# A new issue order for the first six periods of a cross-attention and expert kernel, with fewer dummy matmuls, a later weight load, two sums on GpSimd and a joined router operand

## The chip, the cores and the metric

The kernel runs on one core of a Trainium2 chip. The metric is the device time of one execution in microseconds (us), lower is better; the trace is one profiled execution of the program.

## The reference

There are 8 batches of 256 tokens of width 128. Each goes through a cross-attention with 8 heads of 16 channels, whose softmax runs over the heads and not over the keys, and through a layer of 8 experts of which the two with the highest logits are weighted in.

```python
# attention, q from _layernorm(x), k and v from ctx_1024
scores = einsum('bhqd,bhkd->bhqk', q, k) / sqrt(16)
attn = softmax(scores, axis=1)            # over the 8 heads
ctx = einsum('bhqk,bhkd->bhqd', attn, v)
x = x + ctx @ W_O.T
# experts, on xn = _layernorm(x)
logits = xn @ Wr + br
gates = softmax(top-2 of logits)
h = relu(einsum('btd,edh->bteh', xn, W1) + b1)      # 8 experts, 128 -> 256
x = x + einsum('bte,bteh,ehd->btd', gates, h, W2) + gates @ b2
```

## The kernel before

Each engine runs a list of steps that is written out by hand; semaphores tie the lists together, and nothing reorders them. A batch passes through a pipeline of six stages. In period i, batch i gets its k projection, batch i-1 its q and v, batch i-2 its scores and batch i-3 the rest of its attention, and batches i-4 and i-5 their experts. From period 6 on all engines loop over `period(i)`; the first periods are a list of their own, `beginning()`, on each engine.

Scores come in four units `u` per batch of 128 keys by 128 queries by 8 heads. One unit takes these steps. TensorE's `scores` (or `first_scores` for batch 0) fills one of two buffers `score_ps`; VectorE's `head_max` takes the maximum over the heads; TensorE's `subtract_max` adds its negative; ScalarE's `exponentiate` writes `e_sb`. The sum over heads is made by TensorE with an identity for the four units of batch 0 (`head_sum`, line L351, eight matmuls) and by GpSimd for all others (three additions, L1152 to L1157). ScalarE's `invert_sum` takes logarithm and exponential, VectorE's `normalize` (L911) multiplies. After four units TensorE's `attend_values` and `project_out` follow, then VectorE's `add_residual` and `ln2`, ScalarE's `make_x1n`, TensorE's `transpose_x1n`, `x1T_hi` and `x1T_lo`, and `route` and `expert_up`.

From batch 1 on the heads have to be laid out anew over the partitions. That goes through DRAM on SyncE's queue: `spill_k` writes k and its low part to `k_scratch`, `load_k_stack` reads it into `k_stack`; `spill_q` and `load_q_stack` do the same for q. `scores(b, 0)` waits for both stacks. On the same queue lie the loads of the expert weights w1 (1 MB) and w2 and of the rest of ctx. SyncE issues in program order, and a wait at the head of its list holds all that follows.

w1 is split in a high and a low part: ScalarE's `split_w1(e)` casts, GpSimd's subtracts. `expert_up(0, e)` waits for both. `route` makes the logits from three matmuls for each of two token tiles. `keep_warm(n)` issues n dummy matmuls on the identity (L265). `ln1` makes layer-norm statistics of x on VectorE, and `ln1_rest` finishes them on GpSimd; in the list they stand in five calls, for batches 0, 1, 2, 3 and 4 together, and 5 to 7 together.

## Time and profile before

| what | value |
|---|---|
| median of 3 runs | 211.72 us (211.19 to 213.55) |
| profiled execution | 210.83 us |
| its span, first to last instruction | 209.0 us |
| TensorE busy | 199.0 us, 95% of the span |
| VectorE busy | 166.0 us, 79% |
| ScalarE busy | 132.3 us, 63% |
| GpSimd busy | 110.0 us, 53% |
| granted TensorE clock, mean | 1.000 (2.4 GHz) |

Some 1.8 us of the profiled execution lie outside its span. A busy TensorE need not run at its peak: ends of matmuls are modelled, and one group's busy time reaches a little into the next group's start. The loop over periods starts on TensorE at 81.44 us, with the transposes of batch 5; of batches 0 and 1 the `beginning` lists hold the most, and each later period takes some 22 us.

### The profile page before, as it was taken

The page shows a single profiled execution, that of the slowest core. Times are in us where ns is not written, and L with a number is a line of the kernel's source. Part 1 is how long each engine was busy: PE and PEld are TensorE (multiplying, and loading weights), DVE is VectorE, ACT ScalarE, POOL GpSimd, SP SyncE. Part 2 cuts the span into 40 slices and gives each one's busy share as a digit, 9 for nine tenths or more (in the row PEclk, how much of TensorE's full clock was granted, in tenths as well). Part 3 has the DMA queues.
Part 4 walks back from the last instruction along what each step waited for, and adds up shares of the span by engine and source line. Part 5 has one row for each costly group of instructions (what it writes and reads, how often), then busy time and mean ns, then how long its engine had stood idle before and what let it go on. Part 6 is the DMA issues. An engine that isn't in the chain of part 4 may idle for free.

```text
span 209.0 us, 4976 instructions
## 1 busy us (share of the span) xinstructions
PE 199.0 (95%) x1752; PEld 176.3 (84%) x1752; DVE 166.0 (79%) x445; ACT 132.3 (63%) x316; POOL 110.0 (53%) x132
## 2 busy tenths in 40 slices
PE   6999888698999999999999999999999999999994
PEld 6846775686899889997999799988998999789993
DVE  5398779889789999988888988798989978365542
ACT  2236847796578858687668767575767685345541
POOL 8603657869795475439661966285738672010000
PEclk9999999999999999999999999999999999999999
DMA  6549695725434233424241306050000000000000
GB/s 195 137 137 291 178 266 161 206 86 159 109 102 100 78 100 105 102 75 104 98 106 53 124 14 183 13 175 4 0 3 25 0 2 28 0 3 2 28 0 25
DMA packets 20248, 18.70 MB, mean 89 GB/s; under 512 B 1760, under 2 KB 18688, under 8 KB 20224
## 3 DMA queue, kind: packets, MB, share of 16 engines
q1 hardware_dynamic: 17472, 16.91, 28.2%
q10 hardware_dynamic: 2752, 1.48, 2.7%
q8 instruction: 14, 0.23, 0.4%
q14 instruction: 10, 0.08, 0.1%
HBM read 11.83 MB, written 6.55 MB: 88 GB/s over the span
## 4 chain that ended last, share of the span: by engine, by line
PE 91%; DVE 3%; ACT 2%; issue 1%; POOL 1%; DVEq 0%; POOLq 0%; ACTq 0%
PE y_ps L416 28%; PE h_ps L403 21%; PE score_ps L343 7%; PE misc_ps L362 6%; PE score_ps L331 6%; PE h_ps L351 4%; PE score_ps L265 3%; PE misc_ps L300 2%; PE misc_ps L383 2%; PE score_ps L320 2%; PE score_ps L403 2%; PE misc_ps L371 1%; PE misc_ps L270 1%; PE misc_ps L309 1%; PE misc_ps L289 1%
## 5 line engine op out<-in xcount | busy, mean ns | idle before, releaser
L670 ACT ACTIVATE hT<-h_ps,b_sb 128x256 f32<-128x256 f32 x118 | 49.4, 470 | 34.5 <-PE h_ps L403 33.4
L416 PE MATMUL y_ps<-w_sb,hT 128*128 128x128 f32 x512 | 68.4, 276 | 0.0
L416 PEld LDWEIGHTS y_ps<-w_sb,hT 128*128 128x128 f32 x512 | 63.3, 191 | 3.4 <-issue 2.0
L1152 POOL TENSOR_TENSOR half_sum<-e_sb 128x512 f32<-128x512 f32 x28 | 36.9, 1320 | 34.0 <-ACT e_sb L642 33.6
L911 DVE TENSOR_TENSOR attn<-e_sb,e_rcp 128x1024 f32<-128x1024 f32 x32 | 42.8, 1341 | 3.5 <-ACT e_rcp L653 3.3
L903 DVE TENSOR_REDUCE shift_m<-score_ps 128x128 fp32r<-128x1024 f32 x32 | 38.7, 1213 | 2.4 <-PE score_ps L331 1.2
L403 PE MATMUL h_ps<-x1T_hi,w_lo 128*128 128x256 f32 x118 | 37.7, 320 | 1.3 <-ACT hT L670 0.6
L642 ACT ACTIVATE e_sb<-score_ps 128x1024 f32<-128x1024 f32 x32 | 32.8, 1024 | 5.4 <-PE score_ps L343 5.2
L974 DVE SCALAR_TENSOR_TENSOR acc<-y_ps,gates,acc 128x128 f32<-128x128 f32 x96 | 29.0, 343 | 8.3 <-PE y_ps L416 6.9
L403 PE MATMUL h_ps<-x1T_lo,w_hi 128*128 128x256 f32 x118 | 33.1, 280 | 0.0
L403 PE MATMUL h_ps<-x1T_hi,w_hi 128*128 128x256 f32 x118 | 33.0, 279 | 0.0
L1154 POOL TENSOR_TENSOR quarter_sum<-half_sum 128x256 f32<-128x256 f32 x28 | 27.5, 982 | 2.2
L403 PEld LDWEIGHTS h_ps<-x1T_hi,w_lo 128*128 128x128 f32 x118 | 22.3, 189 | 4.3 <-issue 2.0
L403 PEld LDWEIGHTS h_ps<-x1T_lo,w_hi 128*128 128x128 f32 x118 | 22.4, 190 | 0.3
L403 PEld LDWEIGHTS h_ps<-x1T_hi,w_hi 128*128 128x128 f32 x118 | 22.3, 189 | 0.0
L343 PE MATMUL score_ps<-shift_m,neg_ident 128*128 128x512 f32 x64 | 21.5, 417 | 0.0
L331 PE MATMUL score_ps<-q_stack,k_stack 128*128 128x256 f32 x112 | 19.6, 299 | 1.1 <-issue 1.1
L1157 POOL TENSOR_TENSOR e_sum<-quarter_sum 128x128 f32<-128x128 f32 x28 | 16.6, 592 | 2.2
L1163 POOL TENSOR_TENSOR ln_rstd<-ln_var,neg_half 128x2 f32<-128x2 f32 x8 | 5.7, 708 | 21.2 <-DVE ln_var L870 21.2
L331 PEld LDWEIGHTS score_ps<-q_stack,k_stack 128*128 128x128 f32 x112 | 15.1, 190 | 1.5 <-issue 1.5
L362 PE MATMUL misc_ps<-attn,v_pad 128*32 128x256 f32 x256 | 15.5, 382 | 0.6 <-issue 0.6
L362 PEld LDWEIGHTS misc_ps<-attn,v_pad 128*32 128x32 f32 x256 | 7.7, 109 | 5.9 <-issue 1.0
(113 smaller groups left out, 286.8 us busy)
## 6 DMA issues: line engine op xcount, KB each, us to landing
k_scratch<-k_parts SPq DMA_DIRECT2D x14, 256.0 KB, 2.6
k_stack<-k_scratch SPq DMA_DIRECT2D x14, 256.0 KB, 4.0
q_stack<-q_scratch SPq DMA_DIRECT2D x28, 128.0 KB, 2.7
q_scratch<-q_parts SPq DMA_DIRECT2D x7, 256.0 KB, 2.5
w_sb<-in_w SPq DMA_DIRECT2D x1, 1024.0 KB, 6.5
out_y<-y_out SPq DMA_DIRECT2D x8, 128.0 KB, 1.9
x_all<-in_x ACTq DMA_DIRECT2D x1, 768.0 KB, 6.0
ctxT<-in_ctx_t SPq DMA_DIRECT2D x1, 640.0 KB, 5.5
```

The costliest lines, as they stand in the source:

```text
L331: mm = nc.tensor.matmul(score_ps[:, u % 2, 2 * j * P:(2 * j + 2) * P], k_stack[:, b % 2, j, kt * P:(kt + 1) * P], q_stack[:, b % 2, j, :, ...
L343: mm = nc.tensor.matmul(score_ps[:, u % 2, half * BANK:(half + 1) * BANK], neg_ident[:], m4, start=False, stop=True, skip_group_check=True)
L362: mm = nc.tensor.matmul(misc_ps[32 * g:32 * g + 32, 0:S], v_pad[:, b % 4, kt, h, :], attn[:, b % 2, kt, h, :], start=(odd == 0 and kt == 0 ...
L403: mm = nc.tensor.matmul(hidden(j)[:, c * S:(c + 1) * S], w[:, e, c * P:(c + 1) * P], xt[:, b % 2, :], start=(k == 0), stop=(k == 2))
L416: mm = nc.tensor.matmul(y_ps[:, j % 2, t * D:(t + 1) * D], hT[:, j % 2, c, t * P:(t + 1) * P], w2_sb[:, e * HC + c, :], start=(c == 0), st ...
L642: nc.scalar.activation(e_sb[:, u, :], score_ps[:, u % 2, :], ACT.Exp, scale=SCALE).then_inc(exp_made, 1)
L670: op = nc.scalar.activation(hT[:, j % 2, c, :], hidden(j)[:, c * S:(c + 1) * S], ACT.Relu, bias=b1_sb[:, e * HC + c:e * HC + c + 1])
L903: nc.vector.tensor_reduce(shift_m[:, u % 2, :], score_ps[:, u % 2, :].rearrange("p (h q) -> p q h", h=H), AX.X, ALU.max).then_inc(max_made, 1)
L911: nc.vector.tensor_tensor(attn[:, b % 2, kt, :, qt * P:(qt + 1) * P], e_sb[:, u, :].rearrange("p (h q) -> p h q", h=H), e_rcp[:, u, :].uns ...
L974: op = nc.vector.scalar_tensor_tensor(out=dst, in0=y_ps[:, j % 2, t * D:(t + 1) * D], scalar=gates[:, b % 2, t, e:e + 1], in1=src[:, t, :] ...
L1152: nc.gpsimd.tensor_tensor(half_sum[:], e[:, 0:HQ // 2], e[:, HQ // 2:HQ], ALU.add).then_inc(sum_step, 1)
L1154: nc.gpsimd.tensor_tensor(quarter_sum[:], half_sum[:, 0:HQ // 4], half_sum[:, HQ // 4:HQ // 2], ALU.add).then_inc(sum_step, 1)
```

## The change

The `beginning` lists of TensorE, ScalarE, VectorE and GpSimd are in a new order. Beside that:

- `keep_warm` issues 8, 2 and 1 dummies in place of 12, 5, 1 and 2.
- SyncE loads w1 behind the q stack of batch 1, not ahead of the k stack.
- `PE_SUMS` names the units 1 and 3 of batch 0; the sums of units 0 and 2 go to GpSimd.
- The router's weights stand side by side in `wr_pair`. One matmul of 16 columns and one of 8 take the place of three of 8, and `take_logits` on VectorE adds the two halves in a second instruction. This holds for all eight batches.
- `ln1` and `ln1_rest` are called once for each batch, eight times in all; those of batches 5 to 7 stand much later in the list.
- The transposes of batch 5 in period 6 wait for `v_taken` in place of `b2_added`.

```diff
-    PE_SUMS = 4
+    PE_SUMS = (1, 3,)
...
             spill_k(1)
-            sp.dma_start(w1_sb[:], w1.rearrange("e d h -> d e h")).then_inc(w1_in, 16)
             load_k_stack(1)
             spill_q(1)
             load_q_stack(1)
+            sp.dma_start(w1_sb[:], w1.rearrange("e d h -> d e h")).then_inc(w1_in, 16)
             spill_k(2)
...
                 for t in range(TT):
-                    tok = slice(t * P, (t + 1) * P)
-                    for k, (xt, w) in enumerate(((x1T_hi, wr_lo), (x1T_lo, wr_hi), (x1T_hi, wr_hi))):
-                        mm = nc.tensor.matmul(misc_ps[:, S + t * E:S + (t + 1) * E], xt[:, b % 2, tok], w[:],
-                                              start=(k == 0), stop=(k == 2), skip_group_check=True)
+                    tok, at = slice(t * P, (t + 1) * P), S + 2 * t * E
+                    nc.tensor.matmul(misc_ps[:, at:at + 2 * E], x1T_hi[:, b % 2, tok], wr_pair[:].rearrange("p k e -> p (k e)"),
+                                     start=True, stop=False, skip_group_check=True)
+                    mm = nc.tensor.matmul(misc_ps[:, at:at + E], x1T_lo[:, b % 2, tok], wr_pair[:, 0, :],
+                                          start=False, stop=True, skip_group_check=True)
...
-                    transpose_xn(coming, b2_added, coming - 3)
+                    transpose_xn(coming, *((v_taken, 5) if i == 6 else (b2_added, coming - 3)))
...
             def beginning():
+                project_v(0, None, 0)
                 project_k(0, None, 0)
-                project_v(0, None, 0)
-                keep_warm(5)
+                keep_warm(2)
                 transpose_xn(0, None, 0)
                 keep_warm(1)
                 project_q(0, xnT_taken, 1)
+                project_v(1, v_taken, 1)
                 project_k(1, k_first_made, 1)
-                keep_warm(2)
                 first_scores(0)
...
-            keep_warm(12)
+            keep_warm(8)
...
-                                        br_sb[:].unsqueeze(1).to_broadcast([P, TT, E]), ALU.add).then_inc(logits_made, 1)
+                parts = misc_ps[:, S:S + 2 * TT * E].rearrange("p (t k e) -> p t k e", k=2, e=E)
+                nc.vector.tensor_tensor(logits_part[:], parts[:, :, 1, :], br_sb[:].unsqueeze(1).to_broadcast([P, TT, E]),
+                                        ALU.add).then_inc(logits_step, 1)
+                dve.wait_ge(logits_step, b + 1)
+                nc.vector.tensor_tensor(logits[:], parts[:, :, 0, :], logits_part[:], ALU.add).then_inc(logits_made, 1)
```

The first place is SyncE's queue at the exchange of batch 1 (`k_stack`, `q_stack`), where `w_sb` is w1 and `ctxT` the rest of ctx.

```order
 L242 DMA ctxT<-in_ctx_t 128x256
 L196 DMA k_scratch<-k_parts 256x1x256 x2
-L244 DMA w_sb<-in_w 128x8x256
 L210 DMA k_stack<-k_scratch 64x4x256 x2
 L201 DMA q_scratch<-q_parts 128x512
 L223 DMA q_stack<-q_scratch 32x4x256 x4
+L247 DMA w_sb<-in_w 128x8x256
 L196 DMA k_scratch<-k_parts 256x1x256 x2
 L249 DMA ctxT<-in_ctx_t 128x5x256
```

The load of w1 leaves the exchange of batch 1 and stands at the head of that of batch 2.

The second is TensorE around `scores(1, 0)`, which waits for `q_stack_in1`. Here L351 and L352 are `head_sum`, L343 and L344 `subtract_max`, L331 and L332 `scores`, L289 the q projection, L276 the transposes of xn. Before:

```order
L289 MATMUL misc_ps<-xnT,w_qkvo 128x256 [waits xnT_taken]
L343 MATMUL score_ps<-shift_m,neg_ident 128x512 [waits max_made]
L343 MATMUL score_ps<-shift_m,neg_ident 128x512
L351 MATMUL h_ps<-e_sb,ident 128x128 [waits exp_made,log_made]
L351 MATMUL h_ps<-e_sb,ident 128x128 x7
L331 MATMUL score_ps<-q_stack,k_stack 128x256 [waits exp_made,q_stack_in1,k_stack_in1]
L331 MATMUL score_ps<-q_stack,k_stack 128x256 x3
L351 MATMUL h_ps<-e_sb,ident 128x128 [waits exp_made,log_made]
L351 MATMUL h_ps<-e_sb,ident 128x128 x7
L309 MATMUL y_ps<-w_qkvo,ctxT 128x128 [waits ctx1_in,v_taken]
L309 MATMUL y_ps<-w_qkvo,ctxT 128x128
L331 MATMUL score_ps<-q_stack,k_stack 128x256 [waits exp_made]
```

Now:

```order
L344 MATMUL score_ps<-shift_m,neg_ident 128x512 [waits max_made]
L344 MATMUL score_ps<-shift_m,neg_ident 128x512
L332 MATMUL score_ps<-q_stack,k_stack 128x256 [waits exp_made,q_stack_in1,k_stack_in1]
L332 MATMUL score_ps<-q_stack,k_stack 128x256 x3
L289 MATMUL misc_ps<-xnT,w_qkvo 128x256 [waits xnT_taken]
L352 MATMUL h_ps<-e_sb,ident 128x128 [waits exp_made,log_made]
L352 MATMUL h_ps<-e_sb,ident 128x128 x7
L344 MATMUL score_ps<-shift_m,neg_ident 128x512 [waits max_made]
L344 MATMUL score_ps<-shift_m,neg_ident 128x512
L332 MATMUL score_ps<-q_stack,k_stack 128x256 [waits exp_made]
L332 MATMUL score_ps<-q_stack,k_stack 128x256 x3
```

`scores(1, 0)` has moved ahead of the q projection of batch 2, and of the two sums that stood around it one is left, behind it.

The third is VectorE at the same place. L903 and L902 are `head_max`, L911 and L910 `normalize`, L875 and L874 low parts, L836 to L843 (now L835 to L842) `ln1`, L897 and L899 the split of the router's weights. Before:

```order
L903 TENSOR_REDUCE shift_m<-score_ps 128x128 [waits scores_done]
L911 TENSOR_TENSOR attn<-e_sb,e_rcp 128x8x128 [waits rcp_made] x2
L897 CAST wr_hi<-wr_sb 128x8 [waits small_in]
L899 TENSOR_TENSOR wr_lo<-wr_sb,wr_hi 128x8 [waits wr_hi_made]
L875 TENSOR_TENSOR q_parts<-misc_ps,q_parts 128x256 [waits q_hi_made]
L911 TENSOR_TENSOR attn<-e_sb,e_rcp 128x8x128 [waits rcp_made]
L903 TENSOR_REDUCE shift_m<-score_ps 128x128 [waits scores_done]
L911 TENSOR_TENSOR attn<-e_sb,e_rcp 128x8x128 [waits rcp_made]
L903 TENSOR_REDUCE shift_m<-score_ps 128x128 [waits scores_done]
```

Now:

```order
L902 TENSOR_REDUCE shift_m<-score_ps 128x128 [waits scores_done]
L835 BN_STATS ln_stats<-x_all 128x6 x2
L839 BN_AGGR ln_mv<-ln_stats 128x2 [waits ln1_step]
L839 BN_AGGR ln_mv<-ln_stats 128x2
L842 TENSOR_SCALAR ln_var<-ln_mv 128x2 [waits ln1_step]
L902 TENSOR_REDUCE shift_m<-score_ps 128x128 [waits scores_done]
L910 TENSOR_TENSOR attn<-e_sb,e_rcp 128x8x128 [waits rcp_made]
L874 TENSOR_TENSOR q_parts<-misc_ps,q_parts 128x256 [waits q_hi_made]
L910 TENSOR_TENSOR attn<-e_sb,e_rcp 128x8x128 [waits rcp_made] x2
L902 TENSOR_REDUCE shift_m<-score_ps 128x128 [waits scores_done] x2
L855 TENSOR_TENSOR x<-misc_ps,x_all 128x256 [waits wo_done]
L902 TENSOR_REDUCE shift_m<-score_ps 128x128 [waits scores_done]
```

The first `head_max` of batch 1 now stands ahead of the `normalize` of units 1 to 3 of batch 0, where one stood between units 2 and 3. The last one stands between the residual (L855) and `ln2`, which used to follow each other; and the split of the router's weights has moved on, to a place between the first `head_max` of batch 2 and `x1T_lo` of batch 0.

## Rows read from the trace of the kernel before

**Rows 1.** Windows of the trace: width, each engine's busy us (instructions), clock, DMA share, GB/s.
```profile
10.85:38.92 28.07, 23.93 (x167) 16.84 (x166) 23.52 (x56) 16.90 (x40) 14.13 (x19) 1.00 0.76 212
38.92:81.44 42.52, 41.72 (x376) 37.00 (x377) 38.35 (x93) 31.19 (x76) 30.37 (x37) 1.00 0.39 115
81.44:103.78 22.34, 22.34 (x208) 20.38 (x207) 19.51 (x52) 16.95 (x42) 12.54 (x15) 1.00 0.29 79
```

**Rows 2.** TensorE in order of time, the start: start us, busy us, line, operation, tiles.
```profile
1.61 4.99 PE L265 MATMUL score_ps<-ident 128*128 128x128 f32 x24 [1.61 <-POOL ident L1219]
...
7.32 1.28 PE L265 MATMUL score_ps<-ident 128*128 128x128 f32 x10
...
10.93 1.13 PE L320 MATMUL score_ps<-q_wide,k_first 64*128 64x512 f32 x4
```

**Rows 3.** SyncE's DMA queue in order of time: issue start, issue us, line.
```profile
11.71 1.28 SPq L196 DMA_DIRECT2D k_scratch<-k_parts  x2
...
15.34 1.29 SPq L210 DMA_DIRECT2D k_stack<-k_scratch  x2
...
16.85 0.43 SPq L201 DMA_DIRECT2D q_scratch<-q_parts  x1
...
22.11 1.76 SPq L223 DMA_DIRECT2D q_stack<-q_scratch  x4
...
23.97 1.22 SPq L196 DMA_DIRECT2D k_scratch<-k_parts  x2
...
29.26 0.55 SPq L201 DMA_DIRECT2D q_scratch<-q_parts  x1
...
33.30 1.74 SPq L223 DMA_DIRECT2D q_stack<-q_scratch  x4
```

**Rows 4.** Windows of the trace, the second exchange through DRAM.
```profile
23.00:33.00 10.00, 8.28 (x82) 6.86 (x81) 8.13 (x14) 6.61 (x18) 5.98 (x5) 1.00 0.91 250
```

**Rows 5.** TensorE in order of time, batches 0 to 2.
```profile
26.41 0.71 PE L331 MATMUL score_ps<-q_stack,k_stack 128*128 128x256 f32 x4 [1.09 <-issue]
...
30.92 1.93 PE L362 MATMUL misc_ps<-attn,v_pad 128*32 128x256 f32 x32 [0.62 <-issue]
...
39.06 0.38 PE L403 MATMUL h_ps<-x1T_hi,w_lo 128*128 128x256 f32 x1 [0.47 <-DVE x1T_lo L875]
...
39.86 0.66 PE L331 MATMUL score_ps<-q_stack,k_stack 128*128 128x256 f32 x4
```

**Rows 6.** The chain of waits in order of time: start, us, what.
```profile
23.53 1.78 PE h_ps L351 x16
...
40.02 0.50 PE score_ps L331 x4
```

**Rows 7.** VectorE in order of time: the router's split, a low part, two back-to-back pairs.
```profile
24.47 0.70 DVE L897 CAST wr_hi<-wr_sb 128x8 fp32r<-128x8 f32 x1
...
25.29 0.42 DVE L875 TENSOR_TENSOR q_parts<-misc_ps,q_parts 128x256 fp32r<-128x256 f32 x1
...
35.86 2.36 DVE L903 TENSOR_REDUCE shift_m<-score_ps 128x128 fp32r<-128x1024 f32 x2 [0.20 <-PE score_ps L331]
...
47.73 2.32 DVE L911 TENSOR_TENSOR attn<-e_sb,e_rcp 128x1024 f32<-128x1024 f32 x2
```

**Rows 8.** GpSimd in order of time, first and last step of one sum.
```profile
32.06 1.30 POOL L1152 TENSOR_TENSOR half_sum<-e_sb 128x512 f32<-128x512 f32 x1
...
34.24 0.46 POOL L1157 TENSOR_TENSOR e_sum<-quarter_sum 128x128 f32<-128x128 f32 x1
```

**Rows 9.** Windows of VectorE: layer-norm statistics for one batch, then for three.
```profile
14.93:15.98 1.05, 0.90 (x6) 1.00 0.75 213
31.87:34.16 2.29, 2.22 (x14) 1.00 0.27 89
```

**Rows 10.** TensorE in order of time, the router of batch 2 and what follows it.
```profile
86.03 0.25 PE L300 MATMUL misc_ps<-wr_lo,x1T_hi 128*128 128x8 f32 x1
...
86.70 0.37 PE L403 MATMUL h_ps<-x1T_hi,w_lo 128*128 128x256 f32 x1
```

More of the change, by code:

```diff
@@ L514, in beginning @@
                 project_out(0, heads_taken, 1)
-                project_v(2, x1_made, 1)
-                scores(1, 2)
                 scores(1, 3)
-                transpose_x1n(0, v_taken, 3)
-                subtract_max(1, 2)
+                subtract_max(1, 3)
+                scores(2, 0)
+                scores(2, 1)
+                transpose_x1n(0, x1_made, 1)
+                subtract_max(2, 0)
+                route(0, x1T_lo_made, 1)
                 expert_up(0, 0)
-                scores(2, 0)
@@ L542, in beginning @@
-                project_out(1, b2_added, 1)
+                project_out(1, heads_taken, 2)
+                expert_up(0, 3)
+                project_k(4, x1_made, 2)
+                subtract_max(2, 3)
+                expert_up(0, 4)
                 expert_down(0, 3)
+                scores(3, 0)
+                gated_b2(0, k_lo_made, 4)
                 expert_up(0, 5)
-                project_k(4, x1_made, 2)
+                project_v(3, b2_added, 1)
                 expert_down(0, 4)
-                scores(3, 0)
+                transpose_x1n(1, v_taken, 4)
@@ L548, in beginning @@
+                expert_down(0, 5)
                 expert_up(0, 6)
-                expert_down(0, 5)
-                transpose_x1n(1, k_lo_made, 4)
-                subtract_max(2, 3)
+                transpose_xn(4, x1T_lo_made, 2)
+                subtract_max(3, 0)
+                scores(3, 1)
+                route(1, xnT_taken, 5)
+                expert_down(0, 6)
                 expert_up(0, 7)
-                route(1, x1T_lo_made, 2)
-                expert_down(0, 6)
-                subtract_max(3, 0)
@@ L789, in beginning @@
-                make_x1n(1)
+                exponentiate(2, 3)
+                take_xnT(4)
                 relu(0, 6)
-                take_x1T_hi(1)
+                invert_sum(2, 2)
                 relu(0, 7)
-                exponentiate(2, 3)
-                invert_sum(2, 2)
-                take_xnT(4)
+                take_q_hi(4)
+                exponentiate(3, 0)
                 relu(1, 0)
-                take_v(3)
+                invert_sum(2, 3)
+                exponentiate(3, 1)
```

337 lines of the change are left out of this document (168 added, 169 removed).

## The prediction

> **What bounds the kernel now.** I read the windows by stage first, then each engine in order of time, then SyncE's queue. From 81.44 us on TensorE has no gap: in the period shown it is busy for all of its 22.34 us, VectorE for 19.51 [rows 1]. There only work taken from TensorE shortens anything. Ahead of that lie two stretches with gaps. From 10.85 to 38.92 us TensorE is busy for 23.93 of 28.07 us, so 4.1 us are idle; from 38.92 to 81.44 it is busy for 41.72 of 42.52, 0.8 us idle, while VectorE has 42.52 - 38.35 = 4.2 us of slack [rows 1]. In the first of the two the end is set by a chain across engines and by the exchange through DRAM: `scores(1, 0)` starts at 26.41, 3.0 us after the last of the four q stack loads was issued (22.11 + 3 x 0.44 = 23.43) [rows 3, 5], and the 1.09 us in front of it are put down to issue, where nothing else that the trace follows was late.
>
> I follow three marks: the start of `scores(1, 0)` (26.41), of `expert_up(0, 0)` (39.06), and of period 6 (81.44).
>
> **The start.** The first 24 dummy passes (12 dummies) take 4.99 us, 0.21 each, the next ten 1.28 us, 0.13 each, up to 8.6 us, where the first transposes of xn follow; `first_scores(0)` comes at 10.93 [rows 2]. With eight dummies the first row ends 8 x 0.21 = 1.7 us earlier, and three fewer of the second take 0.8 us out of it. The projections then wait for their data instead, so I take 1.3 us, not 2.5: `first_scores(0)` at about 9.6. The bounds are 0 and 2.5.
>
> **The exchange of batch 1.** The low part of k, ready just before 11.71 [rows 3], now stands on VectorE behind the first `head_max` (1.2 us [rows 7]), and its high part on ScalarE behind the second `take_xnT`. I get 12.5 us for the spill of k, 0.8 later than before. Then w1 is out of the way. Before, k stack loads went out 3.6 us behind the spill, the q spill at 16.85, and its data took until 22.11, 5.3 us; the same step in the next exchange took 4.0 [rows 3]. Now: k stack 12.5 + 3.4 = 15.9, q spill behind it at 17.2, landed 3.6 us later at 20.8 (bounds 2.5 and 4.0 after it), and `scores(1, 0)` 26.41 - 22.11 = 4.3 us after the first q stack load, at about 25.0. That is 1.4 us gained; it could be 0 to 2.5.
>
> This gain doesn't reach `attend_values(0)`, before at 30.92, 4.5 us behind `scores(1, 0)` [rows 5]. VectorE now holds three `normalize` and a low part of q behind `head_max(1, 0)`: 0.7 for the scores, four times 1.2 and 0.3 to 0.4, together 5.8 us [rows 5, 7], so 30.8. The two sums that left TensorE took 2 x 1.8 = 3.6 us of its time [rows 6], but TensorE waits in this stretch anyway. On GpSimd a sum takes 34.24 + 0.46 - 32.06 = 2.6 us [rows 8], and both fit into its idle time there (28.07 - 14.13 = 13.9 us [rows 1]); unit 0's is done some 4 us before VectorE asks. I price this move at nothing; without the wait for the stack it would be worth up to 3.6.
>
> **The exchange of batch 2.** Here w1 has been put in. The spill of k goes out at 23.97, the q stack at 33.30 [rows 3], and from 23 to 33 us the DMA engines are 91% busy at 250 GB/s [rows 4]. So this exchange has no room: 1 MB more at 250 GB/s is 4.2 us, less the 0.9 us of idle share, 3.3. It starts 22.11 - 20.8 = 1.3 us sooner, so the q stack loads go out at 33.3 - 1.3 + 3.3 = 35.3 and `scores(2, 0)` can start at 35.3 + 4.3 = 39.6. Before, it started at 39.86 [rows 5], behind `expert_up(0, 0)`; there the stack, at 37.6, was never waited for. Now it stands ahead of `transpose_x1n(0)`, `route(0)` and `expert_up(0, 0)`, and TensorE is there at about 37.1: from 30.8, 1.9 us of `attend_values`, two `subtract_max`, the heads and `project_out` make 34.4, and the residual, `head_max(1, 3)` and `subtract_max(1, 3)` 2.7 more. So 2.5 us of new wait, bounds 0 and 4. w1 itself, issued at 22.6, has 4.2 us of data and lands by about 28; its first user on ScalarE stands behind `exponentiate(1, 0)`, near 29.5, so that costs nothing. The Trainium skill ("DMA: Bandwidth & Descriptors", section "Queues, rings and completion order") says that each DMA engine consumes descriptors of a queue in ring order. By that rule the spill of k waits for the whole of w1, which gives the 4.2 us with nothing taken off, and 212.4 as the time; the trace agrees as far as it goes, the q spill behind w1 having taken 5.3 us against 4.0 [rows 3].
>
> What follows: 39.6, scores 0.5, `head_max(2, 0)` 1.2, the router's split 25.29 - 24.47 = 0.8, a low part 0.4 [rows 7], `route` 0.45 and three hand-overs of 0.15 give `expert_up(0, 0)` at 43.3 against 39.06, 4.2 us later. Without the stack's wait it would be 41.3, because `ln2(0)` has also slid behind a `head_max`.
>
> **Work already done at that mark.** By the order TensorE has then issued five pieces more than before: `scores(2, 0)` and `(2, 1)`, `subtract_max(1, 3)` and `(2, 0)`, each at about 0.5 [rows 6], and `route(0)`, 0.67 [rows 10]; one projection of four passes (0.4) is still to do, and 0.2 is saved in `route(1)`. Together 2.0 + 0.67 + 0.2 - 0.4 = 2.4 us less lies ahead. Before, 81.44 - 39.06 = 42.4 us lay between the marks, 0.8 of them idle. Now 42.4 - 0.8 - 2.4 = 39.2, and I allow 0.4 for gaps, 0.2 of it for the transposes of batch 5: they now wait for `take_v(4)` and so for the last two steps of ScalarE's list, while TensorE has one projection and one `expert_down` to cover that. Behind them queue all of period 6. So period 6 starts at 43.3 + 39.6 = 82.9, 1.5 us later.
>
> **The router.** Six matmuls take 86.70 - 86.03 = 0.67 us, 0.11 each, though they have 8 columns [rows 10]; their weights are what is loaded. Four take 0.45, with 16 columns no more. That is 0.22 us for each of the six batches in full periods, 1.3 us. The second addition on VectorE is a small one, covered by 22.34 - 19.51 = 2.8 us of slack a period [rows 1]; without that cover it would cost its own length for each batch. Nothing else changes behind period 6. The bounds are 0 and 1.5.
>
> **The norms.** One batch takes 1.05 us, three together 2.29 [rows 9]. The three calls of batches 5 to 7 (3.15 us) move from before 34.16 to behind 43, and all separate calls cost VectorE 1.5 us more. They fill most of its 4.2 us of slack there.
>
> **Sum.** +1.5 - 1.3 = +0.2 us on a span of 209.0; outside it nothing changes (1.8 us), so 211.0 for a profiled execution. The median before lies 0.9 above its profiled execution, and I expect the same of the new one up to half of that: 211.5 us. On the median that is no change. From no change a measurement of this kernel tells about 1%, 2.1 us.
>
> **Rivals.**
> 1. The exchange is not the bound (faster). If w1 flows in gaps, or slower transfers were due to what is now gone, `scores(2, 0)` is not waited for and `expert_up(0, 0)` comes at 41.3: 2.0 us less, 209.5. If `scores(1, 0)` also comes near its early bound, VectorE's idle time shrinks and part of the 3.6 us of the sums shows: 208.0. For it speaks that 1 MB fits easily before anything uses w1; against it the 91% of rows 4. Chance 0.24.
> 2. VectorE becomes the bound (slower). Behind `x1T_lo(0)` it has 38.35 us of work as before, plus 3.15 for the norms and 0.3 for the router, less 2.3 already done: 39.5 us in a stretch of 82.9 - 43.0 = 39.9. It decides from the point at which VectorE waits for more than 0.4 us in there; before it waited 4.2. If it still waits for 3, period 6 starts 2.6 us later: 214.1. Against it: much of its waiting was for a TensorE that had less done. Chance 0.16.
> 3. The dummies were needed (slower). The granted clock reads 1.00 (2.4 GHz) in all rows, yet the pace of the first passes is 0.21 us and later 0.13. If the quick pace came from the number of passes and not with time, the projections and `first_scores` would run some 15 passes at 0.1 us more: 1.5 us at the start, 0.7 of it hidden by VectorE: 212.5. Chance 0.06.
> 4. The new order does nothing for the full periods, because VectorE or ScalarE holds the router's saving: 212.8. Chance 0.04.
>
> **How the numbers follow.** My forecast has a chance of 0.50 and a range of its own of 210.2 to 212.9. Faster by over 1% (below 209.6) is most of rival 1 and little else: 0.21. Slower by over 1% (above 213.8) is two thirds of rival 2 and a tail of the others: 0.15. Within 1%: 0.64. The range goes to 208.3 and 214.0.
>
> **What the profile would show.** `first_scores(0)` near 9.6 us; `scores(1, 0)` near 25.0 with an idle TensorE of 3 to 4 us in front of it; `attend_values(0)` near 30.8; SyncE's q stack loads of batch 2 near 35.3 and TensorE idle ahead of `scores(2, 0)`; `expert_up(0, 0)` near 43.3; period 6 at 82.9 and periods of 22.1 in place of 22.3 us. I am wrong on the exchange if those loads go out before 33; and on VectorE if it has under 1 us of idle time from 43 to 83 us.

## The result, and the profile after

The changed kernel takes 220.0 us, median of four runs (218.6 to 220.6), against 211.6 before: a ratio of 1.037, 95% interval 1.029 to 1.045. It is slower by 3.7%; I had forecast 211.5 us and no change. The profiled execution took 220.1 us, its span is 218.1. The kernel before was measured again beside every group of experiments; each ratio below goes against those runs. Where an execution stands apart as slow, the ratio leaves it out, and the median in us keeps it.

The rows for TensorE on the page of the profile, by fortieths of the span (5.45 us each), of the changed kernel:

```profile
PE   7888288389998999999999999999999999999994
...
PEclk9999679655999999999999999999999999999999
```

Before, the granted clock was at full speed in every slice. Now it drops in the fifth and sixth slice and again from the eighth to the tenth. Windows of the trace after, first around the two drops, then the two stretches in full:

```profile
23.00:24.00 1.00, 0.00 (x0) 0.00 (x0) 0.00 (x0) 0.31 (x1) 0.00 (x0) 0.64 0.92 271
...
30.00:31.00 1.00, 1.00 (x9) 0.95 (x8) 0.89 (x1) 0.18 (x1) 0.00 (x0) 0.95 1.12 395
40.00:41.00 1.00, 0.00 (x0) 0.00 (x0) 0.85 (x1) 0.62 (x1) 1.00 (x1) 0.67 0.85 232
...
54.00:55.00 1.00, 1.00 (x9) 0.96 (x9) 1.00 (x2) 0.69 (x2) 0.00 (x0) 1.00 0.00 0
```
```profile
24.00:30.00 6.00, 4.17 (x17) 4.02 (x18) 2.94 (x4) 0.39 (x1) 0.00 (x0) 0.50 0.89 267
41.00:54.00 13.00, 10.79 (x40) 9.19 (x41) 7.26 (x18) 6.23 (x17) 12.04 (x17) 0.50 0.28 83
```

The clock goes from 1.00 to 0.50 (from 2.4 to 1.2 GHz) while TensorE stands still, comes back near 30 us and, the second time, only at 54. In those 19 us the engine is busy for 14.96 us at half speed; if the same passes take half of it at full speed, some 7.5 us of its time are stretch (an estimate), part of it beside waits of its own.

TensorE in order of time, after; these rows answer to [rows 2, 5]:

```profile
9.55 1.13 PE L321 MATMUL score_ps<-q_wide,k_first 64*128 64x512 f32 x4
...
25.84 1.19 PE L332 MATMUL score_ps<-q_stack,k_stack 128*128 128x256 f32 x4 [4.48 <-issue]
...
27.67 3.11 PE L352 MATMUL h_ps<-e_sb,ident 128*128 128x128 f32 x16
...
33.07 1.93 PE L363 MATMUL misc_ps<-attn,v_pad 128*32 128x256 f32 x32
...
38.83 0.73 PE L344 MATMUL score_ps<-shift_m,neg_ident 128*128 128x512 f32 x2 [1.32 <-DVE shift_m L902]
42.20 2.04 PE L332 MATMUL score_ps<-q_stack,k_stack 128*128 128x256 f32 x8 [2.64 <-issue]
...
47.52 0.56 PE L404 MATMUL h_ps<-x1T_hi,w_lo 128*128 128x256 f32 x1
```

`first_scores(0)` comes at 9.55, `scores(1, 0)` at 25.84 with 4.48 us of idle time in front, `attend_values(0)` at 33.07, `scores(2, 0)` at 42.20 behind 2.64 us, `expert_up(0, 0)` at 47.52, 8.46 later than before. In the first stretch at the lower clock the 16 passes of the sum at 27.67 take 3.11 us, against 1.95 before.

VectorE, then SyncE's queue, after; they answer to [rows 7] and [rows 3]:

```profile
27.07 1.22 DVE L902 TENSOR_REDUCE shift_m<-score_ps 128x128 fp32r<-128x1024 f32 x1 [5.63 <-PE score_ps L332]
...
43.43 1.22 DVE L902 TENSOR_REDUCE shift_m<-score_ps 128x128 fp32r<-128x1024 f32 x1 [2.58 <-PE score_ps L332]
...
45.00 1.19 DVE L898 TENSOR_TENSOR wr_pair<-wr_sb,wr_pair 128x8 fp32r<-128x8 f32 x1
```
```profile
21.41 1.76 SPq L223 DMA_DIRECT2D q_stack<-q_scratch  x4
23.22 0.43 SPq L247 DMA_DIRECT2D w_sb<-in_w  x1
23.75 1.22 SPq L196 DMA_DIRECT2D k_scratch<-k_parts  x2
...
32.56 1.28 SPq L210 DMA_DIRECT2D k_stack<-k_scratch  x2
...
37.82 1.76 SPq L223 DMA_DIRECT2D q_stack<-q_scratch  x4
```

VectorE stands 5.63 us for the first scores of batch 1, and only behind them come the three `normalize` that `attend_values(0)` needs. On the queue the loads of the k stack of batch 2 are issued 8.8 us behind the spill (23.75 to 32.56), those of the q stack at 37.82.

To see where the time lies I cut both spans at the same three marks, `scores(1, 0)`, `expert_up(0, 0)` and `attend_values(3)`, and add a full period. Windows of the kernel before, then after:

```profile
5.00:26.41 21.41, 19.82 (x121) 14.59 (x120) 15.43 (x39) 10.65 (x24) 8.66 (x14) 1.00 0.70 189
26.41:39.06 12.65, 9.62 (x84) 7.33 (x85) 10.70 (x28) 7.87 (x19) 9.16 (x11) 1.00 0.78 217
39.06:95.15 56.09, 55.42 (x487) 50.15 (x487) 50.45 (x124) 41.64 (x102) 36.45 (x44) 1.00 0.36 104
95.15:117.39 22.24, 22.24 (x207) 20.34 (x206) 19.09 (x51) 16.29 (x40) 13.44 (x15) 1.00 0.33 96
```
```profile
5.00:25.84 20.84, 14.84 (x73) 8.91 (x72) 13.29 (x36) 9.18 (x21) 11.45 (x17) 0.94 0.51 139
25.84:47.52 21.68, 16.07 (x94) 12.47 (x95) 15.03 (x21) 10.21 (x21) 13.17 (x17) 0.74 0.68 206
47.52:105.23 57.71, 56.28 (x469) 50.35 (x469) 47.42 (x140) 39.91 (x103) 37.87 (x49) 0.94 0.33 95
105.23:127.27 22.04, 22.04 (x206) 20.14 (x205) 19.22 (x52) 16.30 (x40) 13.46 (x15) 1.00 0.31 91
```

The first piece is 0.6 us shorter, the second 9.0 longer, the third 1.6 longer, and what lies behind 105.23 is 1.0 shorter (112.9 against 113.9 us): +9.1 us of span in all. A full period goes from 22.24 to 22.04. In the second piece TensorE idles 5.6 us where it idled 3.0, and its busy time grows by 6.5, by clock and because the new order puts more of its work ahead of the mark.

### The profile page after: what moved, and what is told of

Same layout as the page of the kernel before. It is cut to its first block, busy times and chain, and to the rows that moved or that the text cites. A ratio compares the mean times of both kernels' runs of the same rounds, so it can differ in the third digit from the quotient of the medians.

```text
span 218.1 us, 4871 instructions
## 1 busy us (share of the span) xinstructions
PE 200.3 (92%) x1686; PEld 174.9 (80%) x1686; DVE 165.6 (76%) x456; ACT 131.4 (60%) x316; POOL 117.2 (54%) x147
## 4 chain that ended last, share of the span: by engine, by line
PE 87%; issue 5%; DVE 4%; ACT 3%; POOL 0%; DVEq 0%; POOLq 0%; ACTq 0%
PE y_ps L417 27%; PE h_ps L404 21%; PE score_ps L332 7%; PE misc_ps L363 7%; PE score_ps L344 7%; PE h_ps L352 2%; PE misc_ps L384 2%; PE score_ps L265 2%; DVE shift_m L902 2%; PE score_ps L404 2%; PE misc_ps L372 1%; ACT e_sb L640 1%; PE misc_ps L289 1%; PE misc_ps L270 1%; PE misc_ps L310 1%
## 5 line engine op out<-in xcount | busy, mean ns | idle before, releaser
L1159 POOL TENSOR_TENSOR half_sum<-e_sb 128x512 f32<-128x512 f32 x30 | 39.0, 1300 | 41.7 <-ACT e_sb L640 41.4
L902 DVE TENSOR_REDUCE shift_m<-score_ps 128x128 fp32r<-128x1024 f32 x32 | 38.7, 1212 | 9.3 <-PE score_ps L332 8.7
L910 DVE TENSOR_TENSOR attn<-e_sb,e_rcp 128x1024 f32<-128x1024 f32 x32 | 42.8, 1337 | 2.1 <-ACT e_rcp L651 2.1
L404 PE MATMUL h_ps<-x1T_hi,w_lo 128*128 128x256 f32 x118 | 38.6, 327 | 0.6 <-ACT hT L668 0.2
L404 PE MATMUL h_ps<-x1T_hi,w_hi 128*128 128x256 f32 x118 | 33.6, 285 | 0.0
L1161 POOL TENSOR_TENSOR quarter_sum<-half_sum 128x256 f32<-128x256 f32 x30 | 29.0, 965 | 2.4
L332 PE MATMUL score_ps<-q_stack,k_stack 128*128 128x256 f32 x112 | 21.4, 319 | 9.0 <-issue 8.1
L332 PEld LDWEIGHTS score_ps<-q_stack,k_stack 128*128 128x128 f32 x112 | 16.9, 209 | 11.0 <-issue 9.1
L404 PEld LDWEIGHTS h_ps<-x1T_hi,w_lo 128*128 128x128 f32 x118 | 22.9, 194 | 3.5 <-issue 2.3
L344 PE MATMUL score_ps<-shift_m,neg_ident 128*128 128x512 f32 x64 | 22.6, 437 | 1.5 <-DVE shift_m L902 1.3
L1170 POOL TENSOR_TENSOR ln_rstd<-ln_var,neg_half 128x2 f32<-128x2 f32 x8 | 6.6, 823 | 19.2 <-DVE ln_var L869 19.2
L344 PEld LDWEIGHTS score_ps<-shift_m,neg_ident 128*128 128x128 f32 x64 | 10.5, 197 | 5.7 <-DVE shift_m L902 3.3
```

The source lines that it names most:

```text
L332: mm = nc.tensor.matmul(score_ps[:, u % 2, 2 * j * P:(2 * j + 2) * P], k_stack[:, b % 2, j, kt * P:(kt + 1) * P], q_stack[:, b % 2, j, :, ...
L344: mm = nc.tensor.matmul(score_ps[:, u % 2, half * BANK:(half + 1) * BANK], neg_ident[:], m4, start=False, stop=True, skip_group_check=True)
L404: mm = nc.tensor.matmul(hidden(j)[:, c * S:(c + 1) * S], w[:, e, c * P:(c + 1) * P], xt[:, b % 2, :], start=(k == 0), stop=(k == 2))
L902: nc.vector.tensor_reduce(shift_m[:, u % 2, :], score_ps[:, u % 2, :].rearrange("p (h q) -> p q h", h=H), AX.X, ALU.max).then_inc(max_made, 1)
L910: nc.vector.tensor_tensor(attn[:, b % 2, kt, :, qt * P:(qt + 1) * P], e_sb[:, u, :].rearrange("p (h q) -> p h q", h=H), e_rcp[:, u, :].uns ...
L1159: nc.gpsimd.tensor_tensor(half_sum[:], e[:, 0:HQ // 2], e[:, HQ // 2:HQ], ALU.add).then_inc(sum_step, 1)
```

## The experiments

Three theories. A: the later w1 load spoils the exchange of batch 2. B: the order lets waits for the stacks stand ahead of work that could run. C: what makes them dear is TensorE's clock, which falls in the gaps.

**e1: w1 back in its old place** (the changed kernel, all else as changed).

```diff
+            sp.dma_start(w1_sb[:], w1...)   # ahead of load_k_stack(1)
-            sp.dma_start(w1_sb[:], w1...)   # behind load_q_stack(1)
```

> The changed kernel with the w1 load back at its old place, ahead of the k stack of batch 1. Theory A (w1 in front of the second exchange holds scores(2, 0)): the q stack loads of batch 2 go out about 10 us after the spill of k, near 34, in place of 14 us after it (37.8), and TensorE no longer waits at scores(2, 0); scores(1, 0) comes 1 to 2 us later than 25.8; time 215 to 217 us. Theory B (it is the new order, in which scores stand ahead of other work, that makes TensorE wait, wherever w1 stands): 219 us or more.

Measured: 220.1 us, ratio 1.042 (1.032 to 1.051). The wait at `scores(2, 0)` is gone, but `scores(1, 0)` moved to 28.31 behind 6.45 us of idle time: the wait has changed its exchange. The time is that of theory B: moving w1 back recovers nothing.

**e2: w1 at the start, on ScalarE's queue** (the changed kernel).

```diff
+                act.dma_start(w1_sb[:], w1...)   # last of ScalarE's first loads
```

> The changed kernel with the w1 load issued last on ScalarE's DMA queue, at about 7 us, when the DMA engines are idle. Theory A: both exchanges run without it, scores(1, 0) near 24.5, the q stack loads of batch 2 near 32, and the granted clock falls at most once; 211 to 214 us. Theory B: TensorE still idles over 3 us ahead of scores(1, 0), the clock still falls there, and the time stays at 216 or more.

Measured: 218.5 us, 1.028 (1.019 to 1.038). SyncE's queue in e2:

```profile
23.58 1.21 SPq L196 DMA_DIRECT2D k_scratch<-k_parts  x2
...
27.23 1.27 SPq L210 DMA_DIRECT2D k_stack<-k_scratch  x2
...
33.47 0.79 SPq L223 DMA_DIRECT2D q_stack<-q_scratch  x2
```

The k stack follows its spill after 3.65 us instead of 8.8, the q stack goes out 4.35 us earlier than in the changed kernel, and `scores(2, 0)` isn't waited for; still only 1.5 us come back, with intervals that overlap. A holds as a mechanism and fails as the cause of most of the loss. The 8.8 us are those of one execution: with w1 in the same place the step took 7.0 us in e3, 7.35 in e5, 7.3 in e6 and 6.9 in e11.

**e3: the gaps filled.** The changed kernel with 20 dummies (two passes each) ahead of `scores(1, 0)` and 12 ahead of `scores(2, 0)`.

```diff
+                keep_warm_h(20, 2)
                 scores(1, 0)
...
+                keep_warm_h(12, 4)
                 scores(2, 0)
```

> The changed kernel with 20 dummy matmuls ahead of scores(1, 0) and 12 ahead of scores(2, 0), in the unused half of the h_ps bank. Theory C (the idle TensorE loses its clock, and that costs as much as the waits): the granted clock stays at 1.00 throughout, scores(1, 0) starts as late as before, near 25.8, and the time falls by 3 to 5 us, to 215 to 217. If the clock cost nothing on the path: within 1 us of 220.

Measured: 217.1 us, 1.023 (1.013 to 1.034): 216.7, 216.9, 217.4 and one of 224.4 us, at mean clocks of 1.000, 0.992, 0.992 and 0.960. The row of the clock on the page of e3, whose profiled execution took 217.4 us, and TensorE in order of time:

```profile
PEclk9999999999997999999999999999999999999999
```
```profile
26.40 0.71 PE L337 MATMUL score_ps<-q_stack,k_stack 128*128 128x256 f32 x4
...
32.21 1.93 PE L368 MATMUL misc_ps<-attn,v_pad 128*32 128x256 f32 x32 [0.53 <-issue]
...
41.21 1.20 PE L337 MATMUL score_ps<-q_stack,k_stack 128*128 128x256 f32 x8
...
45.04 0.36 PE L409 MATMUL h_ps<-x1T_hi,w_lo 128*128 128x256 f32 x1
```

TensorE runs 64 passes more that compute nothing, and the median is 2.9 us lower; three of the four times lie below all four of the changed kernel. The intervals of the two ratios still overlap a little (1.029 to 1.034), so the size is rough; that the clock costs is shown. The two stretches that ran at the lower clock in the changed kernel are now at 1.00: from `scores(1, 0)` to `attend_values(0)` it takes 5.8 us instead of 7.2, from `scores(2, 0)` to `expert_up(0, 0)` 3.8 instead of 5.3. C holds for part of the loss only: `expert_up(0, 0)` still comes 6.0 us later than in the kernel before, with the clock at 1.00 up to 63 us, and the execution at 1.000 throughout is 5.1 us behind the kernel before.

**e4: the kernel before, w1 from ScalarE's queue at the start.**

> The kernel before with the w1 load issued last on ScalarE's DMA queue, at about 7 us. Theory A says that the first exchange of the kernel before gains 2 to 3 us: q stack loads near 19.5 in place of 22.1, scores(1, 0) near 25.3, where TensorE's own work ahead of it ends, and 210.5 to 211.5 us. If w1 cost the first exchange nothing: 211.6.

Measured: 209.9 us, 0.991 (0.987 to 0.995); `scores(1, 0)` at 24.76, `expert_up(0, 0)` at 37.58.

**e5, e6, e7: two places of the order undone.** e5 is exchange 1, e6 exchange 2, e7 both with w1 early. The cut shows TensorE; on VectorE e5 puts `head_max(1, 0)` behind the three `normalize` of batch 0, and e6 `head_max(2, 0)` behind `x1T_low(0)`.

```diff
-                scores(1, 0)
                 project_q(2, xnT_taken, 3)
                 head_sum(0, 3, log_made, 2)
+                scores(1, 0)
...
-                scores(2, 0)
-                scores(2, 1)
                 transpose_x1n(0, x1_made, 1)
                 route(0, x1T_lo_made, 1)
                 expert_up(0, 0)
+                scores(2, 0)
+                scores(2, 1)
```

> The changed kernel with the order of exchange 1 undone: on TensorE `project_q(2)` and batch 0's sum by head stand ahead of `scores(1, 0)` again, on VectorE batch 1's `head_max` stands behind the three normalizations of batch 0. Theory B (the waits for the stacks stand ahead of work that could run) expects TensorE to stand 2 to 2.5 us ahead of `scores(1, 0)` instead of 4.48, VectorE's 5.63 us ahead of line 902 gone or short, `attend_values(0)` near 30.5 instead of 33.07, and 216 to 218 us against the 220.0 of the changed kernel. Theory C (what costs is the clock, which the idle gap takes down) expects more than the 2 us of the gap: the granted clock at 1.00 through 24 to 31 us, and head_sum(0) at 2.0 us instead of 3.1. Theory A (the later w1 load alone) expects 220 within 1, with the wait moved to the next instruction.

> The changed kernel with `scores(2, 0)` and `(2, 1)` and what belongs to them on ScalarE and VectorE moved behind the transposes, the router and `expert_up(0, 0)` of batch 0, in all three orders. Theory B expects the 2.64 us wait for the stack to be covered by that work: `expert_up(0, 0)` at about 44 instead of 47.5, and 217 to 218 us. Theory C adds the clock: where the gap shrinks below 1 us the clock stays at 1.00 behind 41 us and the time comes to 215 to 216; where it still falls, 218. Theory A expects no gain, 219 to 220, because batch 2's stack is the last thing in any order.

> Both of these orders undone in the changed kernel, and w1 loaded from ScalarE's queue at the start instead of SyncE's at 23 us. If order, the place of w1 and the clock that follows from both are the whole of the loss, it comes to the kernel before or below it: 210 to 213 us, with `attend_values(0)` near 29.5, `expert_up(0, 0)` near 41 and period 6 near 83.5, the clock at 1.00 behind the start. A third cause (the sums on GpSimd, the norms, the fewer dummies) would leave it at 214 or above.

Measured: 218.6 us (1.026, 1.014 to 1.039), 220.6 (1.038, 1.028 to 1.048) and 222.4 (1.046, 1.036 to 1.056). B in this form fell with e7, for which it gave 210 to 213 us; the gain of e5, 1.1%, has intervals that overlap. TensorE in e7:

```profile
26.49 0.71 PE L331 MATMUL score_ps<-q_stack,k_stack 128*128 128x256 f32 x4 [1.38 <-issue]
29.09 1.22 PE L343 MATMUL score_ps<-shift_m,neg_ident 128*128 128x512 f32 x2 [1.89 <-DVE shift_m L902]
...
43.44 0.66 PE L282 MATMUL misc_ps<-ident,x1n 128*128 128x128 f32 x2 [3.18 <-ACT x1n L593]
```

The wait ahead of `scores(1, 0)` has shrunk to 1.38 us, but `subtract_max(1, 0)` now waits 1.89 us right behind it, the work that I moved ahead being spent, and the transposes of batch 0 wait 3.18 us for LN2. In a stretch whose work is too little for its waits, moving a piece moves the gap.

**e8: the router part alone**, in the kernel before.

> The kernel before with the router part alone: weights as one operand, four products instead of six in each batch. 0.22 us of TensorE in each of 8 batches, of which the full periods hold most: 1.3 to 1.7 us, 209.9 to 210.3 us against 211.4. If VectorE bounds the full periods (rival 2 of the prediction), no gain.

Measured: 210.2 us, 0.994 (0.990 to 0.999). As priced.

**e9: everything but the order and w1's place.** e9 and e1 differ in the order of the first six periods and in two things that I left with it: e1 has `ln1` and `ln1_rest` once for each batch, and the transposes of batch 5 waiting for `v_taken`.

> Everything of the change but the order and the place of the w1 load: the kernel before with the router part, the fewer dummies and batch 0's sums 0 and 2 on GpSimd (each behind a statistics step on GpSimd). It differs from the first experiment only in the order of the first six periods. If the order is the cause, it stands near the kernel before with the router's gain, 210 to 211.5 us. If the work taken from TensorE (3.9 us of sums, which fill the exchange in the kernel before) or the fewer dummies is the cause, it stands at 214 or above, with TensorE idle 2 us or more ahead of `scores(1, 0)` and the granted clock below 1.00 behind it.

Measured: 212.4 us, 1.004 (1.001 to 1.008), against e1's 1.042 (1.032 to 1.051). So the order, with these two, costs 3.7%, some 8 us. The stages of e9, the first two cut as above:

```profile
5.00:26.18 21.18, 14.91 (x70) 9.04 (x70) 15.52 (x44) 9.20 (x21) 12.98 (x17) 0.94 0.71 194
26.18:40.91 14.73, 11.70 (x85) 9.40 (x85) 11.09 (x28) 8.78 (x22) 10.38 (x14) 0.85 0.74 212
```

They carry a sign of another loss: TensorE idles 6.3 us in the first piece, 4.7 of it in one wait for the q stack ahead of `scores(1, 0)`, and the clock is 0.85 in the second. The profiled execution is one of the two slowest of ten (214.1 us, mean clock 0.966; eight others took 210.8 to 212.9 us with 0.976 to 0.992), so this shows where e9 loses and not how much.

**e10: the sums alone.** The kernel before with batch 0's sums 0 and 2 on GpSimd.

```diff
-                head_sum(0, 0, k_lo_made, 1)
-                head_sum(0, 2, log_made, 2)     # TensorE
+                head_sum(0, 0)
+                head_sum(0, 2)                  # GpSimd
```

> The kernel before with sums 0 and 2 of batch 0 on GpSimd alone. The prediction priced it at 0: 211.4 within 1. The theory that these sums are cover says that the idle time ahead of `scores(1, 0)` grows from 1.09 to some 3 us and the clock falls behind it: 213 to 215.

Measured: 214.0 us, 1.011 (1.003 to 1.018). TensorE in e10:

```profile
26.79 1.19 PE L331 MATMUL score_ps<-q_stack,k_stack 128*128 128x256 f32 x4 [5.19 <-DMA q_stack<-q_scratch]
27.78 3.62 PE L351 MATMUL h_ps<-e_sb,ident 128*128 128x128 f32 x16
```

TensorE had 2 x 1.8 us less to do and the kernel became 1.1% slower, 2.2 us. In the profiled execution the gap ahead of `scores(1, 0)` grew from 1.09 to 5.19 us, the clock fell in it, and the sum behind it took 3.62 us instead of 1.95. This is the slowest of the four executions (216.2 us, mean clock 0.968); the other three took 212.9 to 214.2 us with 0.984 to 0.989, so the clock fell in them too, for a shorter time.

**e11: the sums back on TensorE, in the new order.**

> The changed kernel with all four sums of batch 0 on TensorE again, the third ahead of `scores(1, 0)` in its new order, where TensorE idles 4.48 us. If the missing cover takes the clock down, the gap shrinks to about 2.5 us, the clock holds or falls later, and the time goes to 217 to 218.5 from 220.0, although TensorE has 3.9 us more to do. If the order alone is at fault, 220 within 1.

Measured: 220.4 us, 1.044 (1.036 to 1.052). TensorE in e11, in its profiled execution, the fastest of its four runs at 217.7 us:

```profile
26.08 0.71 PE L332 MATMUL score_ps<-q_stack,k_stack 128*128 128x256 f32 x4 [0.59 <-issue]
...
40.86 2.04 PE L332 MATMUL score_ps<-q_stack,k_stack 128*128 128x256 f32 x8 [2.48 <-issue]
```

The first gap is gone (0.59 us), the second remains, and in the median nothing is won. In this order the sums alone don't help.

**e12: w1 early and the router part**, in the kernel before.

> The kernel before with w1 from ScalarE's queue at the start and the router part, nothing else. Both were measured alone (ratios 0.9912 and 0.9943); if they add, 0.9855, 208.3 us, and it beats both kernels. If the early load has already taken the slack that the router part frees, 209.5 to 209.9.

Measured: 208.8 us, 0.986 (0.981 to 0.992). The two gains add.

**e13: new order ahead of `scores(1, 0)`, old order behind it**, the rest as e9.

> The ninth experiment (old order with the rest of the change) with the new order ahead of `scores(1, 0)` on all four engines (project_v(1) early, first_scores(0) before the transposes of batch 1, k_lo(2) late, no w1 split ahead of exchange 1), and the old order from there on. If the early part costs (its work is spent before the exchange, where it covered TensorE's wait), `expert_up(0, 0)` comes at 43 or later and the time is 216 to 220. If the loss lies behind it, 212 to 213.5, as the ninth.

Measured: 215.7 us, 1.013 (1.003 to 1.023). It lies between e9 (1.004) and e1 (1.042), and the intervals of e13 and e1 don't meet: 2.9% come from what is behind `scores(1, 0)`, 0.9% from what is ahead of it. This split leans to one side. Beside e13 to e16 four of seven runs of the kernel before had a mean clock of 0.984, and their median was 213.5 us, 2 us above the other groups; against its executions at full clock, 211.1 us in this group and in that of e9, e13 stands at 1.021 and e9 at 1.006. In us the medians are 212.4, 215.7 and 220.1: 3.2 us ahead of `scores(1, 0)`, which comes at 28.05 here and at 26.18 in e9, and 4.5 behind it. So both sides cost, and the part behind costs at least as much.

**e14, e15, e17: the chain of batch 0 first.** e14 is e7 with `ln2(0)`, its GpSimd step, `make_x1n(0)` and `expert_up(0, 0)` ahead of the last unit of batch 1; e15 has the four sums on TensorE in addition; e17 is e14 with free work put behind `scores(1, 0)`.

```diff
-                head_max(1, 3)
                 ln2(0)
-                normalize(1, 0)
+                head_max(1, 3)
                 split_wr()
                 x1T_low(0)
+                normalize(1, 0)
```

> The seventh experiment (both scores waits undone, w1 early) and in addition the chain of batch 0 ahead of batch 1's last unit: `ln2(0)` ahead of `head_max(1, 3)` and `x1T_low(0)` ahead of `normalize(1, 0)` on VectorE, `ln2_end(0)` ahead of `head_sum(1, 1)` on GpSimd, `make_x1n(0)` and `take_x1T_hi(0)` ahead of `exponentiate(1, 3)` on ScalarE, `transpose_x1n(0)`, `route(0)` and `expert_up(0, 0)` ahead of `subtract_max(1, 3)` on TensorE. If this chain is the loss behind exchange 1, `expert_up(0, 0)` comes at 41.5 to 42.5 instead of 45.97 and the time is 216 to 218 instead of 222.4. If not, 221 to 223.

> The fourteenth experiment with all four sums of batch 0 on TensorE again, as cover of exchange 1. If missing cover, the chain of batch 0 and w1 are together the loss, it reaches 210 to 213 with the clock at 1.00 through 24 to 50 us and `expert_up(0, 0)` near 39.5. If something else of the new order costs, 215 or above.

> The fourteenth experiment with TensorE's free work put behind `scores(1, 0)`: there stand `head_sum(0, 3)`, `project_v(1)` (taken from the start) and `scores(1, 1)`, and `subtract_max(1, 0)` only then. If the lack of free work in the exchange is what costs, the 2.35 us wait ahead of `subtract_max(1, 0)` (28 to 31 us, with the clock at 0.50 behind it) is gone, `attend_values(0)` comes near 30.5 instead of 32.50, `expert_up(0, 0)` near 41 instead of 43.11, and the time is 1.5 to 3 us under the fourteenth's (its ratio 1.0296): a ratio of 1.015 to 1.023. If the loss is elsewhere in the order, 1.026 or more.

Measured: e14 219.4 us, 1.030 (1.015 to 1.044); e15 221.0, 1.037 (1.024 to 1.050); e17 223.5, 1.061 (1.055 to 1.067). e14 has `expert_up(0, 0)` at 43.11 instead of e7's 45.97, and its ratio is 1.7% lower, with intervals that overlap, part of it by the runs of the kernel before just named. e15 brings nothing on top. e17 is the slowest of all, and TensorE and VectorE show why:

```profile
26.03 1.19 PE L331 MATMUL score_ps<-q_stack,k_stack 128*128 128x256 f32 x4 [3.22 <-issue]
27.02 2.97 PE L351 MATMUL h_ps<-e_sb,ident 128*128 128x128 f32 x16
...
33.10 0.73 PE L343 MATMUL score_ps<-shift_m,neg_ident 128*128 128x512 f32 x2 [2.19 <-DVE shift_m L902]
```
```profile
30.68 1.23 DVE L910 TENSOR_TENSOR attn<-e_sb,e_rcp 128x1024 f32<-128x1024 f32 x1 [3.94 <-ACT e_rcp L650]
31.83 2.35 DVE L902 TENSOR_REDUCE shift_m<-score_ps 128x128 fp32r<-128x1024 f32 x2
```

`head_sum(0, 3)` behind the scores runs at the low clock until 30.0; on its result waits `normalize(0, 3)` (3.94 us), and behind that, by the edit taken over from e5, `head_max(1, 0)`, which `subtract_max(1, 0)` needs. In the kernel before `head_max(1, 0)` stands ahead of `normalize(0, 3)`. The expectation failed, and not by the amount of work but by one place on another engine.

**e16: the fewer dummies alone**, in the kernel before.

> The kernel before with the fewer dummies alone (8, 2, 1, 0 instead of 12, 5, 1, 2). Predicted as part of a start that comes earlier, with the clock at 1.00 from about 5 us: 211.4 within 0.7. If the clock at the start needs them, 212 to 213.

Measured: 210.3 us, 0.989 (0.979 to 0.998), against the same runs of the kernel before as e13 (median 213.5; 211.1 at full clock). The span is 208.4 against 209.0 and the clock 1.00 in every slice. The dummies taken out were not needed.

**e18: the version that the findings point to**, in the kernel before: w1 early, router, fewer dummies; the order and the sums stay.

> The kernel before with w1 from ScalarE's queue at the start, the router part and the fewer dummies; the old order and the old sums. The parts measured alone gave ratios of 0.9912, 0.9943 and 0.9886 (the last against a slower set of runs; its spans differ by 0.6 us, a ratio of 0.997). If they add, 0.983, 207.7 us. If the dummies leave the idle time ahead of `scores(1, 0)` above 2 us, the clock falls there and it is 209 or above.

Measured: 207.9 us, 0.985 (0.982 to 0.987), faster than both kernels. The row of the clock on its page, and TensorE in order of time:

```profile
PEclk9999999999999999999999999999999999999999
```
```profile
24.62 0.71 PE L331 MATMUL score_ps<-q_stack,k_stack 128*128 128x256 f32 x4
...
29.13 1.93 PE L362 MATMUL misc_ps<-attn,v_pad 128*32 128x256 f32 x32 [0.60 <-issue]
...
35.93 0.41 PE L282 MATMUL misc_ps<-ident,x1n 128*128 128x128 f32 x2 [1.41 <-ACT x1n L595]
```

`scores(1, 0)` and `attend_values(0)` come 1.8 us earlier than before, the longest wait of this stretch is 1.41 us, and in the profiled execution the clock is never granted below full speed; the mean clock of the six is 0.999 or 1.000.

## Why the prediction was wrong

**What failed.** Three steps, of which the first weighs most.

The first is that I priced each gap at its own length. I forecast idle gaps of 3 to 4 and of 2.5 us, they came out at 4.48 and 2.64, and behind them I added durations from rows at 2.4 GHz, where the clock was 1.2. No term of mine was a price for the clock behind a gap, and in my third rival the clock stood only as a question of the start. It shows in the sum of the middle, "42.4 - 0.8 - 2.4 = 39.2, and I allow 0.4": between `expert_up(0, 0)` and period 6 lay 91.78 - 47.52 = 44.3 us, 4.7 over the forecast. Windows of the changed kernel:

```profile
47.52:54.00 6.48, 6.25 (x25) 5.71 (x26) 3.21 (x14) 3.14 (x11) 5.91 (x8) 0.50 0.01 3
47.52:91.78 44.26, 42.83 (x361) 37.40 (x362) 34.96 (x108) 29.54 (x78) 29.36 (x39) 0.93 0.35 99
```

By my estimate from them 3.1 us are stretch, half of the 6.25 us at the lower clock; TensorE idles for 1.4 us where I allowed 0.4; and about 0.5 us is work beyond the 39.2. Ahead of the mark, `expert_up(0, 0)` was to come at 43.3 and came at 47.52, 4.2 us late. Of these, 2.6 were there at `scores(2, 0)` (42.20 against 39.6), whose wait for the stack is the third step; 1.6 lie behind it, on a way that took 5.3 us at the lower clock, 3.7 in my forecast and 3.8 in e3 at full clock. The stretch behind the first gap, 1.4 us up to `attend_values(0)`, lies ahead of that wait for the stack, so it can't have set the mark by itself. Together the 4.7 of the middle and these 4.2 are the whole error on the span, 8.9 us. By these estimates some 4.7 of it are clock, 2.6 the stack, and 1.5 idle time and work.

e3 bears this out in part. With the two gaps filled `expert_up(0, 0)` comes at 45.04, and both ways that I had forecast at full clock take what I had forecast. But there the middle still lasts 44.0 us, with 2.4 of them idle and a further drop of the clock between 63.9 and 67 us, and 2.9 us of the time come back in all. What remains is not the lower clock; most of it must be the order's own loss (e1 against e9).

The Trainium skill ("TensorE: Matmul & The Clock Gate", section "HAM oscillation — how this bites in real kernels") describes a wait for DMA after which the next piece of work starts at the lower clock. The trace agrees: clock 0.50 behind the gaps of 4.48 and 2.64 us, the sum at 3.11 us instead of 1.95. I had read the two gaps out of my own numbers and not asked what the clock does in them.

The second is "I price this move at nothing" for the sums. In the order of before it costs 1.1% (e10), with TensorE relieved by 3.6 us. I argued from idle time: where an engine waits anyway, less work saves nothing. True, but less work can cost, because the sums stood in the gap: without them it was 5.19 us long and the clock fell. In the new order, putting them back won nothing in the median (e11), so how much this term cost in the changed kernel isn't shown. The range for this term was 0 to a gain of 3.6; it needed an end below nothing.

The third is the place of w1. The mechanism was right: it goes into exchange 2, holds the spill up and makes `scores(2, 0)` wait. The size was off: q stack loads at 37.82 against 35.3 forecast, which is the 2.6 us above. The spill went out at 23.75 where I had 22.7, and the k stack followed it after 8.8 us, where the 3.9 of the kernel before and my 3.3 for w1 make 7.2. With w1 in the same place this step took 6.9 to 7.35 us in four other kernels (e3, e5, e6, e11), and without w1 3.65 in e2, 3.9 in the kernel before and 4.1 in e7. So in those four w1 costs 3.0 to 3.4 us over the kernel before, as I had taken, and in this execution 4.9; the 4.2 us that went by the rule of the Trainium skill ("DMA: Bandwidth & Descriptors", section "Queues, rings and completion order") lie between. Why this execution took longer isn't known. Taking w1 out of the exchange gains only 1.5 us (e2), because TensorE's own work then brings `expert_up(0, 0)` no earlier than 46.06.

**What held.** `first_scores(0)` at 9.55 (forecast 9.6). `attend_values(0)` "doesn't gain" from the earlier scores, because VectorE holds three `normalize` behind `head_max(1, 0)`: the wait of 5.63 us is there, the mark at 33.07 against 30.8. The router: behind period 6 the span is 126.3 us against 127.6, 1.2 saved against 1.3 forecast, the full period 22.04 us against 22.24, and alone 0.6% (e8). The norms were tried in no run of their own; VectorE has room for them (next paragraph).

**The rivals.** The first (the exchange is not the bound, faster) fell with e2: even without the wait for the stack `expert_up(0, 0)` came at 46.06, not 41.3. The second (VectorE the bound, 214.1) fell: in the third piece of the span VectorE has 57.7 - 47.4 = 10.3 us of slack. The third (dummies needed) fell with e16, the fourth with e8.

**What stays open.** The order, with the separate norms and the wait of batch 5's transposes, costs some 8 us (e1 against e9), on both sides of `scores(1, 0)` (e13). Which of its places hold that isn't shown, nor what those two have of it. Of seven edits inside the new order (e5, e6, e7, e11, e14, e15, e17) none gave a certain gain against the changed kernel and e17 gave a certain loss; most of them only moved a wait to a place that the rows then name. The clock's share is an estimate from one execution, and the rest isn't divided between lost cover and dependences across engines.

## What to carry to other kernels

Where TensorE waits for a round trip through DRAM, the independent work around it is not ballast: list what still stands ahead of and behind each long wait, on every engine, before you remove or reorder a piece, and price a new gap of some microseconds with the clock behind it, not by its length. If two versions differ in a hand-written order, try the other parts of a change in the old order first; here the router part, the fewer dummies and w1 moved the other way are worth 1.5% in it, while the whole change cost 3.7%. A moved wait has to be followed on all engines whose list it stands in.
